# Merging two small loads, reordering the first norms and shortening a peeled pipeline in a two-stage graph network kernel

## The chip, the cores and the metric

The kernel runs on one core of a Trainium2 chip. The metric is the device time of one execution in microseconds (us). An execution before the change takes 4322.72 us (median of three runs, 4320.61 to 4323.55).

## The reference

`x` is 6250 nodes by 256 features, and `src` and `dst` name 100000 edges, sorted by `dst`. Cut to what matters, it computes:

```
h = relu(layernorm(x))
for W_self, W_neigh, b in three layers:          # the last without the relu
    mean = segment_sum(h[src], dst) / degree
    h = relu(h @ W_self + mean @ W_neigh + b)
x = x + h
h = relu(layernorm(x))
Q, K, V = h @ Wq + bq, h @ Wk + bk, h @ Wv + bv  # 8 heads of 32
s = sum(Q * K, per head) / sqrt(32)
a = softmax over each node's in-edges and itself of leaky_relu(s[src] + s[dst])
attn = segment_sum(a * V[src], dst)
h = batch_norm(h + attn @ Wo + bo)
h = batch_norm(h + relu(h @ W1 + b1) @ W2 + b2)
return x + h
```

## The kernel before

Nodes lie in 49 tiles of 128 (the last has 106), edges in 196 blocks (`NB`) of 512 (`BE`); the last block has 160 real edges. `HB` is `NB // 2`, 98.

**Setup.** ACT's queue loads the edge lists (`edges_scalar`, lines 325 to 336) into `raw_i`, one block to a partition, blocks 0 to 97 in the first half and 98 to 195 in the second. For each of `dst` and `src` it issues a DMA of 98 rows (L330), one of 96 rows (L331), one of a single row (L332) and one of 160 numbers (L333); then, behind a wait on GpSimd's memsets, two that fill the last row (L336). A full row is 2 KB. `walk_tables_vector` on DVE waits for all of them (`EDGE_DMAS` times 16 on `edges_in`) and turns the lists into the tables that every later loop reads. SP meanwhile loads `x` in six groups (`load_x`, L540; groups of 4, 9, 12, 12, 8 and 4 tiles), then the first layer's weights, then some edge values at the blocks' ends (L350 to L357; L351 and L352 are 97 rows of 8 bytes each). GpSimd gathers the rows of the first seven blocks straight from `x` (L664).

**First norm.** Each group of `x` ("x", 0 to 5) and each group of the seven gathered blocks ("r", 0 to 3, of 1, 2, 2 and 2 blocks, four rows' sets each) goes through `norm_stats_vector` on DVE, a square root on ACT (`root`, L623), `norm_fold_rows_vector` on DVE and a scaled relu on ACT (`norm`, L630), which for "x" also stores the rows to `h_table` (L634). Everything is in the order written out by hand in `norm_order`, `norm_x_vector`, `norm_ring_vector` and `norm_rows_scalar`: semaphores count along that order. On DVE `walk_tables_vector` stands between group "x" 0 and group "x" 1, and the "r" groups 1 to 3 come behind the first block's one-hots (`behind_first` of the first tile).

**The three layers.** GpSimd gathers the source rows of each block by four indirect DMAs (`gathers`, L763) into a ring of seven slots. It starts on `h_table` when all six stores are in and a slot is free. SP relays (`relay`): it tells PE that a block's rows have landed (L790) and GpSimd that a slot is free (L781). DVE makes one-hot matrices (L842), PE multiplies them with the rows (L897), and per tile come a mean (L952 to L957), transposes (L908, L911) and the dense products (L917, L920).

**The third layer** runs with the start of the attention stage as a software pipeline over tiles (`last_layer_step`). In step t PE sums tile t, finishes tile t-1, and projects tile t-3 (`project_tensor`: L1129 for Q and K, L1131 for V). DVE ends step t with `project_vector(t - 4)` (L1158 to L1172). `pipeline(eng, n, depth, step)` writes the first and last `depth` steps out and loops over those between. A wait of a peeled step on a number below 1 is dropped. In a loop it is always issued, on a register's value.

**Attention and feed-forward.** GpSimd gathers V rows (L1282), first from `vs_early` for five blocks, then from `vs_table`. DVE, ACT and PE do the softmax and the sums batch by batch. Feed-forward and both batch norms follow.

Of the kernel before, what the change touches and what calls it, by code (L numbers as in the profile page):

```python
# [42 lines left out]
def gnn_kernel(nc, x, src, dst, sage_w, sage_b, Wq, bq, Wk, bk, Wv, bv, Wo, bo, W1, b1, W2, b2,  # L43
# [6 lines left out]
    NT = -(-N // P)  # L50
    NP = NT * P
    NL = N - (NT - 1) * P
    NB = -(-E // BE)
# [35 lines left out]
    with ExitStack() as ctx:  # L89
# [230 lines left out]
        first_dmas, late_dmas = setup_dmas[0:3], setup_dmas[3:]  # L320
        FIRST_CONSTS, CONSTS = 16 * len(first_dmas), 16 * (len(setup_dmas) + 3)

        EDGE_DMAS, END_DMAS = 10, 8

        def edges_scalar(act):

            whole, rest = E // BE, E % BE
            for k, of in ((0, dst), (1, src)):
                rows = of[0:whole * BE].rearrange("(b e) -> b e", e=BE)
                act.dma_start(raw_i[:, k, 0, :], rows[0:HB]).then_inc(edges_in, 16)  # L330
                act.dma_start(raw_i[0:HB - 2, k, 1, :], rows[HB:NB - 2]).then_inc(edges_in, 16)  # L331
                act.dma_start(raw_i[HB - 2:HB - 1, k, 1, :], rows[NB - 2:NB - 1]).then_inc(edges_in, 16)  # L332
                act.dma_start(raw_i[HB - 1:HB, k, 1, 0:rest], of[whole * BE:E].rearrange("(a e) -> a e", a=1)).then_inc(edges_in, 16)  # L333
            act.wait_ge(pads_made, 3)
            for k in range(2):
                act.dma_start(raw_i[HB - 1:HB, k, 1, rest:BE], pads[:, 2 * k, rest:BE]).then_inc(edges_in, 16)  # L336
# [209 lines left out]
            sp.dma_start(h_nodes[0:NL, NT - 1, :], x[(NT - 1) * P:N, :]).then_inc(ln_in[-1], 16)  # L546

        raw_groups = [(0, 1)] + [(b, min(b + 2, RAW)) for b in range(1, RAW, 2)]
        norm_order = [("x", 0), ("x", 1), ("x", 2), ("x", 3), ("x", 4), ("x", 5), ("r", 0), ("r", 1), ("r", 2), ("r", 3)]
        assert len(norm_order) == len(ln_groups) + len(raw_groups)  # L550

        def norm_group(kind, g):
# [36 lines left out]
        def norm_x_vector(dve):  # L589

            dve.memset(h_nodes[:, NT - 1, :], 0.0).then_inc(pad_zero, 1)
            norm_stats_vector(dve, "x", 0)
            norm_fold_rows_vector(dve, "x", 0)
            walk_tables_vector(dve)
            norm_stats_vector(dve, "x", 1)
            norm_stats_vector(dve, "x", 2)
            norm_fold_rows_vector(dve, "x", 1)
            norm_stats_vector(dve, "x", 3)
            norm_fold_rows_vector(dve, "x", 2)
            norm_stats_vector(dve, "x", 4)  # L600
            norm_fold_rows_vector(dve, "x", 3)
            norm_stats_vector(dve, "x", 5)
            norm_fold_rows_vector(dve, "x", 4)
            norm_stats_vector(dve, "r", 0)
            norm_fold_rows_vector(dve, "x", 5)
            norm_fold_rows_vector(dve, "r", 0)

        def norm_ring_vector(dve):
            norm_stats_vector(dve, "r", 1)
            norm_stats_vector(dve, "r", 2)  # L610
            norm_fold_rows_vector(dve, "r", 1)
            norm_stats_vector(dve, "r", 3)
            norm_fold_rows_vector(dve, "r", 2)
            norm_fold_rows_vector(dve, "r", 3)

        def norm_rows_scalar(act):
            rows_out = by_partition(tables[0])

            def root(kind, g):
                at, _ = norm_place(kind, g)  # L620
                scale = norm_group(kind, g)[4]
                act.wait_ge(ln_var, at + 1)
                act.activation(scale, scale, ACT.Sqrt).then_inc(ln_sqrt, 1)  # L623

            def norm(kind, g):
                n, rows, _, _, scale, moved = norm_group(kind, g)
                at, _ = norm_place(kind, g)
                act.wait_ge(ln_fold, 2 * at + 2)
                for i in range(n):
                    act.activation(rows[i], rows[i], ACT.Relu, bias=moved[:, i:i + 1], scale=scale[:, i:i + 1]).then_inc(ln_done, 1)  # L630
                if kind == "x":
                    t0, t1 = ln_groups[g]
                    act.wait_ge(ln_done, t1)
                    act.dma_start(rows_out[:, t0:t1, :], h_nodes[:, t0:t1, :]).then_inc(stored0, 16)  # L634

            root("x", 0)
            norm("x", 0)
            root("x", 1)
            root("x", 2)
            norm("x", 1)  # L640
            root("x", 3)
            norm("x", 2)
            root("x", 4)
            norm("x", 3)
            root("x", 5)
            norm("x", 4)
            root("r", 0)
            norm("x", 5)
            norm("r", 0)
            root("r", 1)  # L650
            root("r", 2)
            norm("r", 1)
            root("r", 3)
            norm("r", 2)
            norm("r", 3)
            act.wait_ge(stored0, 16 * len(ln_groups))
# [218 lines left out]
        def sage_tensor(pe, l):  # L875
            if l == 0:
                walk_tables_tensor(pe)
                pe.wait_ge(walk_made, WALKED)
                pe.wait_ge(const_in, FIRST_CONSTS)

                pe.sem_inc(W["onehot_used"], BJ)
            else:
                pe.wait_ge(const_in, CONSTS)
                late_rows_tensor(pe, l)

            idle_ps = banks[:, 3 if l < 2 else 7, :]

            def sums(t):
                b0, b1 = span(pe, t)

                wait(pe, W["mean_made"], since("mean_made", l, t))
                pe.matmul(agg[:, 0:D + 1], zeros[:, 0:P], zeros[:, 0:D + 1], start=True, stop=False)
                with pe.Fori(b0, b1 + 1) as b:
                    pe.wait_ge(W["rows_ready"], since("rows_ready", l, b + 1))
                    for j in range(BJ):
                        pe.wait_ge(W["onehot_made"], since("onehot_made", l, (b + t) * BJ + j + 1))
                        pe.matmul(agg[:, 0:D + 1], onehot[:, j, :], ring[:, (b % SLOTS) * BJ + j, 0:D + 1],  # L897
                                  start=False, stop=False).then_inc(W["onehot_used"], 1)
                    for _ in range(4 if l < 2 else 1):
                        pe.matmul(idle_ps, zeros[:, 0:P], zeros[:], start=True, stop=True)  # L900
                pe.matmul(agg[:, 0:D + 1], zeros[:, 0:P], zeros[:, 0:D + 1], start=False, stop=True).then_inc(W["agg_done"], 1)  # L901

            def turn(t):

                wait(pe, W["lhs_made"], since("lhs_made", l, t))
                pe.wait_ge(W["self_made"], since("self_made", l, t + 1))
                for k in range(KD):
                    pe.transpose(tp[:, KD + k, :], h_self[:, k * P:(k + 1) * P], ident[:])  # L908
                pe.wait_ge(W["mean_made"], since("mean_made", l, t + 1))
                for k in range(KD):  # L910
                    last = pe.transpose(tp[:, k, :], mean[:, k * P:(k + 1) * P], ident[:])  # L911
                last.then_inc(W["turned"], 1)

            def products(t):

                wait(pe, W["h_made"], since("h_made", l, t))
                pe.matmul(dense[:, 0:D], ones_row[:], b_sage[0:1, l, :], start=True, stop=False)  # L917
                pe.wait_ge(W["lhs_made"], since("lhs_made", l, t + 1))
                for k in range(2 * KD):
                    last = pe.matmul(dense[:, 0:D], lhs[:, k, :], w_sage[:, l, k, :], start=False, stop=k == 2 * KD - 1)  # L920
                last.then_inc(W["out_done"], 1)

            def step(t):
                sums(t)
                turn(t)
                products(t)

            def last_layer_step(t):
                if there(t):
                    sums(t)  # L930
                if there(t - 1):
                    turn(t - 1)
                if there(t - 3):
                    turn_normed_tensor(pe, t - 3)
                if there(t - 1):
                    products(t - 1)
                if there(t - 3):
                    project_tensor(pe, t - 3)
            if l == 0:
                first_and_rest(pe, 2 * GS, step)  # L940
                late_ends_tensor(pe)
                with pe.Fori(2 * GS, NT) as t:
                    step(t)
            elif l == 1:
                first_and_rest(pe, NT, step)
            else:
                pipeline(pe, NT, 4, last_layer_step)

        def sage_vector(dve, l):
            def means(t):  # L950
# [173 lines left out]
        def project_tensor(pe, t):  # L1124
            pe.wait_ge(Q["lhs_made"], t + 1)
            wait(pe, Q["taken"], t)
            wait(pe, Q["step"], 4 * t - 3)
            for k in range(KD):
                pe.matmul(qk_ps, lhs_q[:, k, :], w_qkv[:, k, 0:2 * D], start=k == 0, stop=k == KD - 1)  # L1129
            for k in range(KD):  # L1130
# [995 lines left out]
```

## Time and profile before

| | |
|---|---|
| median of three runs | 4322.72 us |
| profiled execution | 4322.72 us, span 4320.9 us from first to last instruction |
| granted TensorE clock, mean | 0.945 |
| busy: PE, DVE, ACT, GpSimd | 82%, 50%, 11%, 70% |
| DMA, mean | 130 GB/s |

The span is what the trace shows; the 1.8 us around it are no part of it. PE's busy time includes products with zeros (L900) whose result nobody reads. GpSimd's busy time leaves out some 0.3 us between two indirect DMAs, so that 70% is a queue that hardly stops.

### The profile page before, as it was taken

What the parts mean: (1) busy time and instruction counts of PE and PEld (TensorE: products, weight loads), DVE (VectorE), ACT (ScalarE), POOL (GpSimd) and SP (SyncE); (2) the same over time, 40 slices, a digit from 0 to 9 for tenths busy, and PEclk for the clock granted to TensorE, in tenths of its full rate; (3) what the DMA queues carried; (4) which work ended last, traced back from release to release, by engine and by line L of the source; (5) the groups of instructions that cost most, each with busy time, mean ns of one, the idle gap of its engine ahead of it and who ended that gap; (6) DMA issues with size and microseconds to landing.
All of it is one profiled execution on the core that took longest, in us unless ns stands there. A gap on an engine that the chain in (4) does not pass through costs nothing. (4 is left out here: it accounts for less than half of the span.)

```text
span 4320.9 us, 79500 instructions
## 1 busy us (share of the span) xinstructions
PE 3542.6 (82%) x15834; PEld 2480.8 (57%) x15925; DVE 2155.8 (50%) x6078; ACT 487.9 (11%) x1111; POOL 3030.0 (70%) x3154
## 2 busy tenths in 40 slices
PE   4888888888988888888888888888777777777798
PEld 2666655555655556565666656665555555555544
DVE  5443333333333333333455555555577777777733
ACT  4000000000000000000010111101011111111122
POOL 5777777777777777777777777776777777777200
PEclk9999999999999999999999999999788989897999
DMA  5344334434344344344444444444655555554411
GB/s 197 119 138 124 120 110 125 124 105 143 106 123 124 104 124 124 104 124 126 128 141 136 138 140 136 139 139 147 168 147 156 147 156 148 159 147 137 127 60 60
DMA packets 284795, 563.69 MB, mean 130 GB/s; under 512 B 104637, under 2 KB 176132, under 8 KB 279690
## 3 DMA queue, kind: packets, MB, share of 16 engines
q0 software_dynamic: 150528, 414.45, 33.6%
q10 hardware_dynamic: 70180, 89.46, 6.2%
q1 hardware_dynamic: 63974, 58.59, 4.4%
q8 instruction: 33, 0.54, 0.1%
q14 instruction: 80, 0.66, 0.0%
HBM read 487.19 MB, written 73.45 MB: 130 GB/s over the span
## 5 line engine op out<-in xcount | busy, mean ns | idle before, releaser
L763 POOL DMA_INDIRECT arena<-h_table,idx_v x2292 | 2182.5, 952 | 731.7 <-issue 693.0
L897 PE MATMUL banks<-arena 128*128 x5856 | 1467.0, 395 | 356.2 <-SPq L790 244.8
L897 PEld LDWEIGHTS banks<-arena 128*128 128x128 f32 x5856 | 1110.7, 195 | 679.6 <-issue 497.8
L842 DVE TENSOR_SCALAR arena<-iota_t,dst_e 128x128 f32<-128x128 f32 x2928 | 853.5, 307 | 795.3 <-PE banks L897 515.2
L1282 POOL DMA_INDIRECT arena<-vs_table,idx_v x764 | 765.6, 1002 | 232.8 <-issue 229.4
L900 PE MATMUL banks<-zeros 128*128 128x512 bf16 x2108 | 585.3, 386 | 4.4 <-issue 0.4
L1500 PE MATMUL banks<-arena 128*128 x1952 | 518.5, 416 | 51.6 <-DVE arena L1844 51.5
L1500 PEld LDWEIGHTS banks<-arena 128*128 128x128 f32 x1952 | 366.4, 199 | 190.7 <-issue 119.2
L952 DVE TENSOR_SCALAR small<-banks 128x1 f32<-128x1 f32 x147 | 23.3, 159 | 674.4 <-PE banks L901 674.4
L900 PEld LDWEIGHTS banks<-zeros 128*128 128x128 bf16 x2196 | 218.7, 100 | 202.0 <-issue 12.7
L1020 ACT ACTIVATE lhs<-banks 128x512 f32<-128x512 f32 x147 | 87.8, 597 | 2137.9 <-PE banks L911 2137.7
L920 PE MATMUL banks<-arena,lhs 128*128 128x256 f32 x1176 | 293.2, 392 | 6.4 <-ACT lhs L1020 0.2
L1844 DVE SCALAR_TENSOR_TENSOR arena<-iota_n,tile_base,dst_e 128x256 f32<-128x256 f32 x488 | 224.2, 483 | 117.3 <-PE banks L1500 117.0
L920 PEld LDWEIGHTS banks<-arena,lhs 128*128 128x128 f32 x1176 | 211.7, 190 | 84.7 <-ACT lhs L1020 61.6
L1839 DVE TENSOR_TENSOR arena<-arena,banks (+1 forms) x196 | 239.1, 1220 | 30.9 <-issue 24.3
L911 PE MATMUL banks<-ident,tiles 128*128 128x128 f32 x294 | 63.3, 298 | 77.4 <-DVE tiles L957 77.4
L830 DVE TENSOR_SCALAR iota_t<-iota_n,tile_base 128x128 f32<-128x128 f32 x147 | 48.2, 328 | 153.7 <-issue 153.7
L917 PE MATMUL banks<-arena,ones_row 1*128 1x256 f32 x294 | 102.5, 428 | 0.0
L1129 PE MATMUL banks<-arena 128*128 128x512 f32 x196 | 92.3, 593 | 2.4 <-DVE arena L1162 2.4
L911 PEld LDWEIGHTS banks<-ident,tiles 128*128 128x128 f32 x294 | 33.3, 145 | 101.0 <-DVE tiles L957 101.0
L1972 PE MATMUL banks<-arena 128*128 (+2 forms) x208 | 86.2, 568 | 1.3 <-DVE arena L1927 1.3
L1982 PE MATMUL banks<-arena 128*128 128x512 f32 (+1 forms) x208 | 86.4, 569 | 0.2 <-DVE arena L1936 0.2
(265 smaller groups left out, 2512.3 us busy)
## 6 DMA issues: line engine op xcount, KB each, us to landing
arena<-h_table,idx_v POOLq DMA_INDIRECT x2292
arena<-dst_dram SPq DMA_DIRECT2D x14, 1792.0 KB
arena<-vs_table,idx_v POOLq DMA_INDIRECT x764
h_table<-arena ACTq DMA_DIRECT2D x11, 1024.0 KB, 7.4
h_early<-arena ACTq DMA_DIRECT2D x10, 1024.0 KB
vs_table<-arena ACTq DMA_DIRECT2D x49, 132.0 KB
x_dram<-arena ACTq DMA_DIRECT2D x49, 128.0 KB
hln_dram<-arena ACTq DMA_DIRECT2D x49, 128.0 KB
```

The costliest lines, as they stand in the source:

```text
L763: pool.indirect_dma_start(ring[:, s * BJ + j, 0:width], None, table, bass.IndirectOffsetOnAxis(idx_v[:, half, n * BJ + j:n * BJ + j + 1], ...
L842: dve.tensor_scalar(onehot[:, j, :], iota_t[:], dst_e[:, bass.ds(b * BJ + j, 1)], None, ALU.is_equal).then_inc(W["onehot_made"], 1)
L897: pe.matmul(agg[:, 0:D + 1], onehot[:, j, :], ring[:, (b % SLOTS) * BJ + j, 0:D + 1], start=False, stop=False).then_inc(W["onehot_used"], 1)
L900: pe.matmul(idle_ps, zeros[:, 0:P], zeros[:], start=True, stop=True)
L911: last = pe.transpose(tp[:, k, :], mean[:, k * P:(k + 1) * P], ident[:])
L917: pe.matmul(dense[:, 0:D], ones_row[:], b_sage[0:1, l, :], start=True, stop=False)
L920: last = pe.matmul(dense[:, 0:D], lhs[:, k, :], w_sage[:, l, k, :], start=False, stop=k == 2 * KD - 1)
L1129: pe.matmul(qk_ps, lhs_q[:, k, :], w_qkv[:, k, 0:2 * D], start=k == 0, stop=k == KD - 1)
L1282: pool.indirect_dma_start(v_ring[:, at, 0:VS], None, table, bass.IndirectOffsetOnAxis(idx_v[:, half, s * BJ + j:s * BJ + j + 1], 0)).then_ ...
L1500: pe.matmul(agg[:, 0:RW], onehot_v[:, j, :], v_ring[:, (b - (k - k % 2) * BB) * BJ + j, :], start=False, stop=False).then_inc(G["a_used"], 1)
L1839: dve.tensor_tensor(v, v, w.broadcast_to([P, BJ, HEADS, C]), ALU.mult).then_inc(G["rows_ready"], 1)
L1844: dve.scalar_tensor_tensor(onehot_v[:, j:j + 2, :], nodes_twice, tile_base[:, bass.ds(t, 1)], ends_of(b * BJ + j), ALU.add, ALU.is_equal). ...
```

## The change

There are three edits.

1. In `edges_scalar` the DMA of 96 rows and the one of a single row behind it become one of 97 rows, for `dst` and for `src`. Eight DMAs instead of ten are waited for.
2. In the first norm the statistics and roots of "r" 0 and "r" 1 move ahead of those of "x" 4 and "x" 5. ACT's relu work keeps its order. "r" 1 leaves `norm_ring_vector`.
3. PE's pipeline of the third layer peels three steps instead of four. The wait of `project_tensor` on DVE's steps becomes 4t instead of 4t-3 (the whole of `project_vector(t - 1)` instead of its first instruction).

```
-        EDGE_DMAS, END_DMAS = 10, 8
+        EDGE_DMAS, END_DMAS = 8, 8
...
-                act.dma_start(raw_i[0:HB - 2, k, 1, :], rows[HB:NB - 2]).then_inc(edges_in, 16)
-                act.dma_start(raw_i[HB - 2:HB - 1, k, 1, :], rows[NB - 2:NB - 1]).then_inc(edges_in, 16)
+                act.dma_start(raw_i[0:HB - 1, k, 1, :], rows[HB:NB - 1]).then_inc(edges_in, 16)
...
-        norm_order = [("x", 0), ("x", 1), ("x", 2), ("x", 3), ("x", 4), ("x", 5), ("r", 0), ("r", 1), ("r", 2), ("r", 3)]
+        norm_order = [("x", 0), ("x", 1), ("x", 2), ("x", 3), ("r", 0), ("r", 1), ("x", 4), ("x", 5), ("r", 2), ("r", 3)]
...
             norm_fold_rows_vector(dve, "x", 2)
+            norm_stats_vector(dve, "r", 0)
+            norm_fold_rows_vector(dve, "x", 3)
+            norm_stats_vector(dve, "r", 1)
+            norm_fold_rows_vector(dve, "r", 0)
             norm_stats_vector(dve, "x", 4)
-            norm_fold_rows_vector(dve, "x", 3)
+            norm_fold_rows_vector(dve, "r", 1)
             norm_stats_vector(dve, "x", 5)
             norm_fold_rows_vector(dve, "x", 4)
-            norm_stats_vector(dve, "r", 0)
             norm_fold_rows_vector(dve, "x", 5)
-            norm_fold_rows_vector(dve, "r", 0)
 
         def norm_ring_vector(dve):
-            norm_stats_vector(dve, "r", 1)
             norm_stats_vector(dve, "r", 2)
-            norm_fold_rows_vector(dve, "r", 1)
...
             norm("x", 2)
+            root("r", 0)
+            norm("x", 3)
+            root("r", 1)
             root("x", 4)
-            norm("x", 3)
             root("x", 5)
             norm("x", 4)
-            root("r", 0)
             norm("x", 5)
             norm("r", 0)
-            root("r", 1)
+            norm("r", 1)
             root("r", 2)
-            norm("r", 1)
...
-                pipeline(pe, NT, 4, last_layer_step)
+                pipeline(pe, NT, 3, last_layer_step)
...
-            wait(pe, Q["step"], 4 * t - 3)
+            wait(pe, Q["step"], 4 * t)
```

## Rows read from the trace of the kernel before

**Rows 1.** GpSimd's waits over the span: total us, times, longest us.
```profile
POOL arena L763 <- issue: 702.7, 2306, 0.3
...
POOL arena L763 <- SPq L781: 38.8, 18, 24.5
POOL arena L1282 <- DMA vs_early<-arena: 12.7, 1, 12.7
```

**Rows 2.** Lines 763 and 1282: duration ns min/median/max, first and last start us.
```profile
L763 POOL DMA_INDIRECT arena<-h_table,idx_v x2292: 942/946/1809, 66.0 to 2994.7; - x191
...
L1282 POOL DMA_INDIRECT arena<-vs_table,idx_v x764: 942/946/4050, 3034.5 to 4031.7; - x191
```

**Rows 3.** Timeline from 0 to 30 us: start us, us, engine, line, op, [idle before <-releaser].
```profile
1.87 0.35 ACTq L332 DMA_DIRECT2D arena<-in_dst_dram  x1
...
11.68 1.23 DVE L402 CAST arena<-arena 98x2048 f32<-98x2048 int32 x1 [2.43 <-DMA arena<-arena]
...
23.51 3.02 DVE L574 BATCH_NORM_STATS2 bn<-arena 128x6 f32<-128x256 f32 x9
```

**Rows 4.** DMA queues from 2.0 to 3.4 us: packets, MB, share of 16 engines.
```profile
q10 hardware_dynamic: 112, 0.20, 40.9%
```

**Rows 5.** DMA queues from 3.4 to 5.35 us.
```profile
q10 hardware_dynamic: 112, 0.20, 35.6%
```

**Rows 6.** DMA queues from 5.82 to 9.82 us.
```profile
q1 hardware_dynamic: 766, 0.78, 67.9%
q10 hardware_dynamic: 245, 0.40, 34.5%
```

**Rows 7.** DMA queues from 20 to 22 us.
```profile
q1 hardware_dynamic: 426, 0.44, 69.2%
q0 software_dynamic: 85, 0.25, 36.2%
```

**Rows 8.** DMA queues from 37.162 to 38.372 us.
```profile
q1 hardware_dynamic: 98, 0.00, 4.6%
```

**Rows 9.** Timeline of SP from 23.2 to 40 us.
```profile
30.40 5.80 SPq L352 DMA_DIRECT2D arena<-in_dst_dram  x1
```

**Rows 10.** Timeline from 30 to 110 us: first norm and the first blocks.
```profile
38.26 2.70 DVE L574 BATCH_NORM_STATS2 bn<-arena 128x6 f32<-128x256 f32 x8
...
44.92 5.99 ACT L630 ACTIVATE arena<-arena,shift,rstd 128x256 f32<-128x256 f32 x12
...
51.78 4.02 ACT L630 ACTIVATE arena<-arena,shift,rstd 128x256 f32<-128x256 f32 x8
...
58.80 2.07 ACT L630 ACTIVATE arena<-arena,bn 128x256 f32<-128x256 f32 x4 [0.41 <-ACT arena L630]
...
72.18 0.93 DVE L842 TENSOR_SCALAR arena<-iota_t,dst_e 128x128 f32<-128x128 f32 x4 [0.41 <-issue]
...
77.31 0.94 POOL L763 DMA_INDIRECT arena<-h_table,idx_v  x1 [6.63 <-SPq L781]
...
90.02 0.94 POOL L763 DMA_INDIRECT arena<-h_table,idx_v  x1 [3.01 <-SPq L781]
```

**Rows 11.** Waits from 2100 to 2990 us, in the third layer.
```profile
PE banks L897 <- SPq L790: 71.1, 38, 2.9
```

**Rows 12.** Timeline from 2500 us: a tile of the third layer.
```profile
2501.05 0.21 DVE L1169 TENSOR_SCALAR s_node<-small 128x8 f32 x1 [0.15 <-DVE small L1166]
2501.22 1.88 PE L1129 MATMUL banks<-arena 128*128 128x512 f32 x4
```

**Rows 13.** Timeline from 2985 us: the end of the third layer.
```profile
3014.79 1.96 PE L1129 MATMUL banks<-arena 128*128 128x512 f32 x4 [1.51 <-DVE arena L1162]
...
3015.51 0.33 DVE L1169 TENSOR_SCALAR s_node<-small 128x8 f32<-128x8 f32 x1
```

**Rows 14.** Timeline from 3026 us: the start of the attention stage.
```profile
3032.03 8.01 DVE L1251 TENSOR_SCALAR arena<-arena,node_id 128x512 f32<-128x512 int32 x20 [1.53 <-DMA vs_table<-arena]
...
3034.53 1.28 POOL L1282 DMA_INDIRECT arena<-vs_table,idx_v  x1 [0.30 <-issue]
```

## The prediction

> **What bounds the kernel now.** I read the waits of GpSimd first, then its two gather lines, then the timeline of the first 110 us, and last the third layer.
>
> GpSimd's waits are the key view [rows 1]. Nearly all its idle time in the three layers is "issue", 0.3 us between two gathers, which belongs to the stream itself. Of real waits there are 38.8 us for free slots, 24.5 of them one wait, and 12.7 us at the hand-over to the attention stage. The gather lines [rows 2] show one stream: from 66.0 to 2994.7 us there are 2323 intervals (2292 gathers from the table and 32 from the early copies, less one), and 2928.7 / 2323 = 1.26 us is one gather of 0.946 us with its 0.3. So the layers take what GpSimd needs, and whatever moves the stream's start moves its end by as much. The attention stage hangs on layer 2's end and so on the same start. The reader is to see that the end of the kernel is set 4250 us earlier: by when GpSimd gets going.
>
> What sets that is the timeline of the start. DVE begins `walk_tables_vector` at 11.68 us, released by the last edge DMA [rows 3]. From there DVE goes without a pause to 23.51, where the statistics of "x" 1 begin, and the norms follow. GpSimd's first gather from the table is at 65.99, released by the slot of block 0; it waits again until 77.31 and 90.02 [rows 10], and then runs. So the edge DMAs stand at the head of the critical path.
>
> **Edit 1, the edge loads.** What it removes is two issues on ACT's queue of about 0.35 us each (one is L332 in [rows 3]); if nothing else changed, the two pad DMAs behind them would start and land up to 0.7 us earlier.
>
> What it adds is a shape. A DMA leaves one packet for each row and one small one for each DMA engine that reports its share done. In 2.0 to 3.4 us the 98-row DMA left 112 packets, 98 + 14 [rows 4]; in 3.4 to 5.35 us the 96-row one left 112, 96 + 16 [rows 5]. So 98 rows went over 14 engines, 7 each, and 96 over 16, 6 each. The kernel already has two loads of 97 rows, though of 8 bytes: L351 and L352 [rows 9]. The first left 98 packets in 37.162 to 38.372 us [rows 8]: 97 + 1. One engine did it all. 97 is prime, and 98 = 14 x 7; the rows say that the number of engines divides the number of rows. So I expect each merged load to put its 97 rows on a single engine, and both loads on the same one, since they are of one shape.
>
> The Trainium skill says so too, and speaks against the edit by it: "DMA: Bandwidth & Descriptors", "Why a DMA increments its semaphore by 16 and not by 1", has the largest number up to 16 that divides the slowest dimension of both sides, and the lowest-numbered engines take the work. Its 127-partition example goes on one engine, as 97 would. The same page gives an engine about 27 GiB/s; by that the 426 KB below would take some 15 us, below the floor from rows.
>
> How long does this take? That engine gets 7 + 97 full rows for `dst` and as many for `src`, 208 rows of 2 KB. Floor: in [rows 4] 40.9% of 16 engines over 1.4 us is 9.2 us for 98 rows, 0.094 us each; 208 of them are 19.5 us. But SP's `x` loads share every engine. Ceiling: in [rows 6] the `src` loads, 13 rows to an engine, took the 4.0 us, 0.31 us a row; 208 would be 64 us. Between them I count the engine's work. A packet of `x` (1 KB) is 0.679 x 64 / 766 = 0.057 us [rows 6]. The engine's part of `x` is 48 full tiles x 8 rows, 53 of the last tile's 106 (two engines by the same rule), and 32 of the weights, 469 packets, 26.6 us. A gather's 4 KB packet is 0.362 x 32 / 85 = 0.136 us [rows 7], 28 raw gathers x 2 = 56 of them, 7.6 us. Together 53.7 us, from 2.2 us on: by 56 nothing is left. If the engine turns between the queues at equal bytes, two packets of `x` go with each row: 208 x (0.094 + 0.114) + 7.6 = 51 us, ending at 53. The shares in [rows 6] and [rows 7] add to 102 and 105%, so packets overlap a little; I take the last row at 50 us, and 45 to 56 as its own range. From the last row to DVE's start it was 11.68 - 9.82 = 1.9 us, kept. DVE then starts at 51.9 instead of 11.7: +40.2 us.
>
> What else is queued there: ACT's later issues may block while the ring is full, as SP's L352 did for 5.80 us behind L351 [rows 9]. ACT's root and relu of "x" 0 come behind them, but have until 51.9. The `x` groups are in the same engine's other queue; group 1 is wanted at 51.9 + 11.8 = 63.7, when the engine is empty. None of this adds. Nothing hides the 40 us: everything on GpSimd from its 66 us on waits for this chain.
>
> **Edit 2, the first norm.** In the old clock. "r" 0 and 1 take 2.0 and 3.6 us of DVE statistics (eight, with aggregation, as from 38.26 [rows 10]). DVE gets to "x" 4 only behind the fold of "r" 0, whose root stands behind ACT's relu of "x" 2: 45.4. It ends there at 49.0, then must fold "r" 1, whose root stands behind the relu of "x" 3, which ends at 50.9 [rows 10]: 52.2. Then the statistics of "x" 5, 2.0 us, to 54.2. ACT has the root of "x" 5 ahead of the relu of "x" 4, so this relu starts at 54.7 instead of 51.78: +2.9. "x" 5 and "r" 0 follow: block 0 is ready at 63.7 instead of 60.9 (58.80 + 2.07), and GpSimd's first gather comes at 68.8. But the "r" 1 relu follows at once, to 67.7, and behind the first one-hots DVE has only "r" 2 and 3, 7.2 us of statistics from 58.0, and their roots, which stand behind ACT's "r" 1 relu: 68.8. Block 1's one-hots come at 69.2 instead of 72.18. PE follows with blocks 1, 2 and 3 in the same steps, so GpSimd's other two starts come 3.0 us earlier, 74.3 and 87.0; block 7's four gathers are done at 73.8. The last of the three sets the stream: -3.0 us. Bounds: -3.0, and +2.9 if the first start should bind, which it doesn't while the third lies where it does.
>
> **Edit 3, the pipeline.** The order of PE's instructions stays; one peeled step becomes a loop step. The new wait holds PE until L1169 of the tile before has ended, 2501.26, where PE's L1129 began at 2501.22 [rows 12]: with a semaphore's way about +0.3 us a tile. PE waited 71.1 us for rows in 38 waits of 890 us [rows 11], up to 2.9 each, so this is hidden. In the written-out tail it costs once or twice the full difference, from 14.79 to 15.84 [rows 13], together some 2 us. The last store to `vs_table` released DVE at 3032.03, and GpSimd wants it only at 3034.2 [rows 14]: 2.2 us of slack. Taken as nothing, at most +2. Without the cover it would be 45 x 0.3 = 13.5 us more.
>
> **The sum**, against the profiled execution's own 4322.72 us, which is also the median: 4322.7 + 40.2 - 3.0 + 0 = 4360 us.
>
> **The rivals.**
> (a) One engine, but the edge rows are served ahead of `x`. For it: a ring that always has work may get more than half the turns. Against: [rows 6], where these rows had a third of the engines. Last row between 22 and 40 us, time 4332 to 4348, middle 4340.
> (b) The merged load spreads, as 2 KB rows might be cut otherwise than 8-byte ones. Then the head moves by -0.7 us and edit 2 by -3.0: 4319 us, no change that can be measured. Against: 98 and 96 rows of 2 KB were split by whole rows. It decides from two engines or more: 97 rows on two would already cost half.
> (c) The new wait of PE makes it the bound of the third layer: 4360 + 15 = 4375 us. Against: [rows 11].
> (d) More is stuck than the edges: SP's issues behind the full ring (weights, the late end values) come after 62 us and hold PE or the relay, or edit 2 costs its +2.9: 4366 to 4385.
>
> **How the numbers follow.** Forecast 0.70, (a) 0.13, (b) 0.06, (c) 0.03, (d) 0.08. 0.2% is 8.6 us, about what a measurement of this kernel can tell from no change. Slower is all but (b) and a sliver of (a): 0.91; same 0.07; faster 0.02. The forecast's own range is 4353 to 4366. The 8-in-10 range reaches into (a) and (d): 4338 to 4374.
>
> **What would show it.** DVE's L402 near 52 us, released by a DMA, is edit 1; if at 11 to 12, (b). The DMA queues between 12 and 48 us should show ACT's queue with some 190 packets where it now has only stores. Relative to L402, GpSimd's first three starts should come +2.8, -3.0 and -3.0 us against 54.3, 65.6 and 78.3. In the third layer PE's L1129 should begin about 0.3 us later after L1162, and GpSimd's waits beyond 100 us stay as they are. The prediction is wrong if the edge rows do not go to one engine, or if that engine serves them in far less than 0.2 us each.

## The result and the profile after

The changed kernel takes 4344.88 us (median of five runs, 4341.93 to 4345.54), against 4322.39 us (4320.61 to 4323.55) for the one before: 1.0051 times as long, 95% interval 1.0037 to 1.0066. That is slower, by 22.5 us, as forecast in kind. It lies inside the 8-in-10 range of 4338 to 4374 us, but 15 us under the forecast value and outside its own range of 4353 to 4366, at the time of rival (a). The profiled run took 4346.55 us with a span of 4344.7, 23.8 us more than before's span. Lines from L332 on stand one number lower than before.

GpSimd's waits (total us, times, longest us), which answer to [rows 1]:

```profile
POOL arena L762 <- issue: 704.0, 2311, 0.3
...
POOL arena L762 <- SPq L780: 59.0, 12, 55.2
POOL arena L1281 <- DMA vs_early<-arena: 12.7, 1, 12.7
...
POOL arena L1281 <- DMA vs_table<-arena: 4.1, 1, 4.1
```

Its two gather lines (duration ns, first and last start us), which answer to [rows 2]:

```profile
L762 POOL DMA_INDIRECT arena<-h_table,idx_v x2292: 942/946/1806, 95.5 to 3015.6; - x191
...
L1281 POOL DMA_INDIRECT arena<-vs_table,idx_v x764: 942/946/6032, 3058.3 to 4055.2; - x191
```

The stream is unchanged between its ends: the same "issue" of 0.3 us, now 2311 times. Its first gather starts 29.5 us later, its last only 20.9 us later (3015.6 against 2994.7). So 8.6 us are won back at the start. Then 2.9 us are lost between the last gather of the layers and the first from `vs_table` (42.7 us against 39.8), behind which stands a wait of 4.1 us that is new. What comes after moves by 23.5 us (its last gather) to 23.8 us (the end).

The timeline from 0 to 62 us (start us, us, engine, line, op, idle before and its releaser) shows the start of the chain, [rows 3] before:

```profile
4.69 17.64 ACTq L332 DMA_DIRECT2D arena<-in_src_dram  x1
...
38.97 1.23 DVE L401 CAST arena<-arena 98x2048 f32<-98x2048 int32 x1 [12.99 <-DMA arena<-arena]
...
50.75 3.02 DVE L573 BATCH_NORM_STATS2 bn<-arena 128x6 f32<-128x256 f32 x9
```

DVE's walk begins at 38.97 instead of 11.68, +27.3 us, and the statistics of "x" 1 keep their distance to it (11.8 us both times). Three windows of the DMA queues (packets, MB, share of 16 engines) show why. The first is 3.4 to 5.35 us, that of [rows 5]:

```profile
q1 hardware_dynamic: 568, 0.51, 90.6%
q10 hardware_dynamic: 20, 0.04, 6.5%
```

The second is 12 to 20 us:

```profile
q1 hardware_dynamic: 1263, 1.28, 50.2%
q0 software_dynamic: 388, 1.07, 40.4%
q10 hardware_dynamic: 43, 0.08, 2.9%
```

Where ACT's queue (q10) moved 112 packets in 1.95 us, it now moves 20, and then 43 in 8 us: 0.19 us a row, on 2.9% of the sixteen engines, less than half of one engine. That fits one engine which carries the rows and spends over half its time on the other queues. The third is 20 to 22 us:

```profile
q0 software_dynamic: 63, 0.17, 31.9%
q10 hardware_dynamic: 13, 0.02, 3.3%
q1 hardware_dynamic: 13, 0.01, 1.9%
```

SP's queue (q1) with `x` moved 426 packets in this window before [rows 7] and now moves 13, exactly as many as ACT's. The two together took 5.2% of sixteen engines, 0.83 of one. So `x` too has come down to the pace of one engine, and that engine takes one `x` packet (0.047 us) for one packet of the edges (0.081 us).

The timeline from 60 to 125 us, the first blocks, which answer to the second half of [rows 10]:

```profile
81.41 4.04 ACT L629 ACTIVATE arena<-arena,shift,rstd 128x256 f32<-128x256 f32 x8
...
88.34 6.00 ACT L629 ACTIVATE arena<-arena,bn 128x256 f32<-128x256 f32 x12 [0.41 <-ACT arena L629]
...
90.77 3.79 PE L896 MATMUL banks<-arena 128*128 x8 [35.32 <-SPq L789]
...
95.52 0.94 POOL L762 DMA_INDIRECT arena<-h_table,idx_v  x1 [55.20 <-SPq L780]
95.61 0.97 DVE L841 TENSOR_SCALAR arena<-iota_t,dst_e 128x128 f32<-128x128 f32 x4 [0.41 <-issue]
96.11 2.00 PE L896 MATMUL banks<-arena 128*128 x8 [0.28 <-DVE arena L841]
...
111.05 0.94 POOL L762 DMA_INDIRECT arena<-h_table,idx_v  x1 [0.78 <-SPq L780]
```

Counted from the walk's start, GpSimd's first start comes at +56.5 us (before +54.3), block 1's one-hots at +56.6 (before +60.5), its last start at +72.1 (before +78.3). GpSimd no longer waits at its second start. There is a second gain beside the earlier one-hots: block 1's products take 2.00 us. Before, the timeline had them at half that speed, after a pause of PE:

```profile
72.68 3.79 PE L897 MATMUL banks<-arena 128*128 x8 [5.96 <-DVE arena L842]
```

The windows view (us, busy us of PE, PEld, DVE, ACT, POOL, granted clock, DMA share, GB/s) gives the granted clock there, before:

```profile
72.00:77.00 5.00, 4.32 (x10) 2.98 (x11) 2.08 (x8) 5.00 (x11) 0.00 (x0) 0.50 0.00 0
```

and after:

```profile
95.00:98.00 3.00, 2.72 (x12) 1.72 (x11) 2.00 (x8) 3.00 (x7) 1.89 (x2) 1.00 0.14 44
```

0.50 is the level of 1.2 GHz, 1.00 that of 2.4 GHz. From block 1's products to block 2's, PE took 5.09 us before and takes 2.70 now.

The end of the third layer, on the timeline from 3015 us, which answers to [rows 13] and [rows 14]:

```profile
3036.78 3.00 PE L1128 MATMUL banks<-arena 128*128 128x512 f32 x4 [2.64 <-DVE s_node L1168]
...
3039.57 1.71 PE L1130 MATMUL banks<-arena 128*128 128x256 f32 x4
...
3043.53 2.93 PE L1128 MATMUL banks<-arena 128*128 128x512 f32 x4 [2.03 <-DVE s_node L1168]
...
3046.26 1.78 PE L1130 MATMUL banks<-arena 128*128 128x256 f32 x4
...
3058.28 1.07 POOL L1281 DMA_INDIRECT arena<-vs_table,idx_v  x1 [4.14 <-DMA vs_table<-arena]
```

The waits before the last two projections are 2.64 and 2.03 us, now on DVE's L1168 (before 1.51 and 0.89, on L1162), and the products behind them are longer, 3.00 and 2.93 us against 1.96, and 1.71 and 1.78 against 1.03. The windows view gives their clock:

```profile
3036.00:3040.00 4.00, 3.22 (x5) 1.50 (x6) 1.09 (x5) 0.60 (x1) 3.09 (x4) 0.69 0.60 168
```

Before, the two windows of 4 us from 3014 to 3022 have 1.00. The balance in the profiled runs: +27.3 at the walk (edit 1), -6.3 from there to GpSimd's third start (edit 2), so the stream's end at +20.9; the hand-over +2.9; the end of the kernel 23.8 us later.

### The profile page after: what moved, and what is told of

Same layout as the page of the kernel before. It is cut to its first block and busy times, and to the rows that moved or that the text cites. A ratio compares the mean times of both kernels' runs of the same rounds, so it can differ in the third digit from the quotient of the medians.

```text
span 4344.7 us, 79597 instructions
## 1 busy us (share of the span) xinstructions
PE 3546.9 (82%) x15924; PEld 2471.0 (57%) x15925; DVE 2157.0 (50%) x6078; ACT 488.6 (11%) x1111; POOL 3027.9 (70%) x3154
## 5 line engine op out<-in xcount | busy, mean ns | idle before, releaser
L899 PE MATMUL banks<-zeros 128*128 128x512 bf16 x2196 | 604.5, 385 | 0.0
L1128 PE MATMUL banks<-arena 128*128 128x512 f32 x196 | 98.5, 626 | 4.7 <-DVE s_node L1168 4.7
```

## The experiments

They ran on other chips. The kernel before itself takes some 6350 to 6430 us there instead of 4322. In the experiments' profiles the mean granted clock is 0.78 to 0.79 (0.945 before), and GpSimd waits 1443 to 1495 us for slots (38.8 in [rows 1]). A difference of a few us is not to be had from such totals, so the verdicts rest on rows of the start and of the tail. Where a total is given, it is the median of 10 or 12 runs beside the kernel before on the same chip. The others are single runs. "First start" is GpSimd's first gather from `h_table`, "one-hots" are those of block 1, and both are often counted from the start of DVE's walk.

**e1_edges: edit 1 alone.**

```
-        EDGE_DMAS, END_DMAS = 10, 8
+        EDGE_DMAS, END_DMAS = 8, 8
...
-                act.dma_start(raw_i[0:HB - 2, k, 1, :], rows[HB:NB - 2]).then_inc(edges_in, 16)
-                act.dma_start(raw_i[HB - 2:HB - 1, k, 1, :], rows[NB - 2:NB - 1]).then_inc(edges_in, 16)
+                act.dma_start(raw_i[0:HB - 1, k, 1, :], rows[HB:NB - 1]).then_inc(edges_in, 16)
```

> Edit 1 alone. Theory 1: the 97 rows of both loads go through one DMA engine, each row waiting its turn beside x's; DVE's first step of the walk comes at 39 us instead of 11.7 and everything behind keeps its distances: 4322.4 + 27.3 = about 4350 us. Rival: the late start in the changed kernel comes in part from the new order of the norms; then the first step of the walk comes clearly before 39 us, and the time stays under 4345 us.

6450.22 us, 1.0029 times before (95% 1.0005 to 1.0054): 24.6 us longer, with an interval of 3 to 35 us. The timeline:

```profile
4.68 17.61 ACTq L332 DMA_DIRECT2D arena<-in_src_dram  x1
...
39.23 1.23 DVE L401 CAST arena<-arena 98x2048 f32<-98x2048 int32 x1 [13.62 <-issue]
...
92.99 0.94 POOL L762 DMA_INDIRECT arena<-h_table,idx_v  x1 [52.41 <-SPq L780]
...
99.73 3.79 PE L896 MATMUL banks<-arena 128*128 x8 [6.85 <-DVE arena L841]
```

Edit 1 by itself gives the whole delay of the walk. From the walk on, the old distances stand (first start +53.8, before +54.3), and block 1's products take 3.79 us, as before.

**e2_norms and e2_norms_b: edit 2 alone**, on two chips. The diff is that of `norm_order`, `norm_x_vector`, `norm_ring_vector` and the ACT list in the change; only the line that matters most:

```
-        norm_order = [("x", 0), ("x", 1), ("x", 2), ("x", 3), ("x", 4), ("x", 5), ("r", 0), ("r", 1), ("r", 2), ("r", 3)]
+        norm_order = [("x", 0), ("x", 1), ("x", 2), ("x", 3), ("r", 0), ("r", 1), ("x", 4), ("x", 5), ("r", 2), ("r", 3)]
```

> Edit 2 alone. Theory 1 (order and clock): block 1's one-hots come early enough that PE has no long gap before block 1, its clock stays at full and the products of block 1 take 2.0 us instead of 3.8; the third start of GpSimd comes 6 us earlier against the walk, 4316 us. Rival (order alone): only the 3 us of the one-hots are won, 4319 us.

> Edit 2 alone once more, as the first chip took some 2100 us longer for every kernel and its times can't tell a few us. Theory 1 (order and clock): PE's clock stays full for block 1 and the third start of GpSimd comes 6 us earlier against the walk, 4316 us. Rival (order alone): 3 us, 4319 us.

Totals: 0.9997 (0.9978 to 1.0016) and 1.0009 (0.9984 to 1.0034), no difference. The timeline of the first, from 60 to 95 us:

```profile
81.70 0.94 POOL L763 DMA_INDIRECT arena<-h_table,idx_v  x1 [40.53 <-SPq L781]
81.79 0.97 DVE L842 TENSOR_SCALAR arena<-iota_t,dst_e 128x128 f32<-128x128 f32 x4 [0.41 <-issue]
82.29 2.00 PE L897 MATMUL banks<-arena 128*128 x8
...
87.54 0.29 DVE L842 TENSOR_SCALAR arena<-iota_t,dst_e 128x128 f32<-128x128 f32 x1 [2.83 <-PE banks L897]
...
90.39 0.32 DVE L842 TENSOR_SCALAR arena<-iota_t,dst_e 128x128 f32<-128x128 f32 x1 [2.57 <-remote]
...
93.25 0.49 DVE L842 TENSOR_SCALAR arena<-iota_t,dst_e 128x128 f32<-128x128 f32 x2 [2.54 <-remote]
...
94.00 0.94 POOL L763 DMA_INDIRECT arena<-h_table,idx_v  x1 [2.60 <-SPq L781]
```

Against e3_pipe, which has the old order, and counted from each one's walk: first start +70.3 against +67.6, one-hots +70.4 against +73.8, block 1's products 2.00 us against 3.44. Edit 2 does in the start what the changed kernel shows; on the second chip block 1's products take 2.04 us. What it wins is gone again at block 3, whose one-hots wait twice for some 2.5 us on "remote", a releaser outside the core's own record, which the profile after does not have there. So these totals neither confirm nor deny its 6.3 us.

**e3_pipe: edit 3 alone.**

```
-                pipeline(pe, NT, 4, last_layer_step)
+                pipeline(pe, NT, 3, last_layer_step)
...
-            wait(pe, Q["step"], 4 * t - 3)
+            wait(pe, Q["step"], 4 * t)
```

> Edit 3 alone. Theory 1: the wait on the whole of DVE's projection steps costs in the written-out tail, PE's gaps lower its clock there, the last store to vs_table comes some 5 us later and uses up 2 us of slack; GpSimd waits 3 to 4 us there: 4325 to 4327 us. Rival: the tail has slack enough and the 4.1 us wait in the changed kernel comes from something else: 4322 us, no wait.

6428.78 us, 0.9994 (0.9971 to 1.0017). The last two projections:

```profile
4495.80 1.96 PE L1129 MATMUL banks<-arena 128*128 128x512 f32 x4 [2.26 <-issue]
...
4500.82 1.95 PE L1129 MATMUL banks<-arena 128*128 128x512 f32 x4 [1.98 <-issue]
```

The waits are near those of the changed kernel (2.64 and 2.03); the products are not slower. So slow products are no fixed consequence of the wait.

**e4_norms_pipe: edits 2 and 3 together**, without edit 1 (their diffs as above).

> Edits 2 and 3 without edit 1. If the three edits add up: 4322.4 - 6.3 + 3 = about 4319 us. If they act on each other (x arriving late together with the new order of the norms): several us off this.

6429.68 us, 1.0000 (0.9979 to 1.0020). First start 81.81, one-hots 81.90: the start of e2. Waits of 2.52 and 2.13 us in the tail, and the last L1129 takes 3.57 us. In these rows the edits don't disturb each other.

**e5_dst_only: the merged load for `dst` alone**, to tell an engine that serves rows one after another from a fixed delay.

```
-        EDGE_DMAS, END_DMAS = 10, 8
+        EDGE_DMAS, END_DMAS = 9, 8
...
+                if k == 0:
+                    act.dma_start(raw_i[0:HB - 1, k, 1, :], rows[HB:NB - 1]).then_inc(edges_in, 16)
+                else:
+                    act.dma_start(raw_i[0:HB - 2, k, 1, :], rows[HB:NB - 2]).then_inc(edges_in, 16)
+                    act.dma_start(raw_i[HB - 2:HB - 1, k, 1, :], rows[NB - 2:NB - 1]).then_inc(edges_in, 16)
```

> Only the dst load merged to 97 rows, the src load as before. Theory (one engine, 208 rows in some 36 us, 0.17 us a row): the engine has 7 + 97 + 7 + 6 = 117 rows, the last at about 22 us, and DVE's first step of the walk comes at 23 to 25 us, half way between 11.7 and 39. Rival (the late start comes from ACT's blocked issues, not from the engine's rows): nothing blocks ACT with one such load, and the walk begins before 15 us.

```profile
23.59 1.23 DVE L405 CAST arena<-arena 98x2048 f32<-98x2048 int32 x1 [8.12 <-DMA arena<-arena]
```

Less the 1.9 us from last row to DVE and the 2.2 us at the start, both taken from the kernel before, that is 19.5 us for the 7 + 97 + 7 + 6 = 117 rows of the loaded engine, 0.167 us each. The changed kernel has 38.97 - 4.1 = 34.9 us for 208 rows, 0.168 each. The delay is proportional to the rows on the one engine. ACT's queue isn't held here (its longest issue is 1.66 us).

**e6_two_parts: the same 97 rows as 48 and 49**, still two issues.

```
-                act.dma_start(raw_i[0:HB - 2, k, 1, :], rows[HB:NB - 2]).then_inc(edges_in, 16)
-                act.dma_start(raw_i[HB - 2:HB - 1, k, 1, :], rows[NB - 2:NB - 1]).then_inc(edges_in, 16)
+                act.dma_start(raw_i[0:48, k, 1, :], rows[HB:HB + 48]).then_inc(edges_in, 16)
+                act.dma_start(raw_i[48:HB - 1, k, 1, :], rows[HB + 48:NB - 1]).then_inc(edges_in, 16)
```

> The same 97 rows as two loads of 48 and 49 rows, no load of a single row. Theory (the number of engines divides the number of rows): 16 and 7 engines, at most 3 + 7 = 10 rows of 2 KB on one engine in place of 97; the walk begins at 12 to 14 us. Rival (these rows are slow for another reason, the last rows of the list or the partitions they go to): it begins near 39 us as in the changed kernel.

```profile
12.17 1.24 DVE L402 CAST arena<-arena 98x2048 f32<-98x2048 int32 x1 [3.29 <-DMA arena<-arena]
```

The same bytes go to the same rows, and the delay is 0.5 us instead of 27. Even that is none that can be told: with the old edge loads the walk starts between 11.34 and 12.27 us in eight profiles. It is the count 97 that costs. "DMA: Bandwidth & Descriptors" of the Trainium skill, section "Why a DMA increments its semaphore by 16 and not by 1", takes the largest number up to 16 that divides the slowest dimension of both sides; by that rule 48 rows go to 16 engines and 49 to 7. This run agrees with it as far as the walk's start can.

**e7_x_behind: edit 1, with SP's `x` groups 1 to 5 held until the edges are in**, to measure what the other queue takes of the loaded engine.

```
+            sp.wait_ge(edges_in, 16 * EDGE_DMAS)
             for g in range(1, len(ln_groups)):
                 load_x(sp, g)
```

> Edit 1 with the loads of x groups 1 to 5 held back until the edges are in. Theory (each row waits one turn of x's queue): without x the engine needs 0.09 us a row and the gathers' share, 208 rows in 20 to 27 us, and the walk begins at 24 to 30 us instead of 39. Rival (the engine is slow by itself on such rows, whatever else is queued): it stays at 37 us or more.

```profile
4.52 11.16 ACTq L332 DMA_DIRECT2D arena<-in_src_dram  x1
...
27.51 1.27 DVE L401 CAST arena<-arena 98x2048 f32<-98x2048 int32 x1 [8.47 <-DMA arena<-arena]
```

208 rows in 27.51 - 4.1 = 23.4 us, 0.113 each. With `x` beside them (e1, same edit) the walk starts 11.7 us later. Some 3.3 of these are gathers, whose queue took 28.5% of the engines in e1 from 2 to 37 us. Add the 32 packets of `x` group 0 that this run has too, some 1.5 us, and `x` comes to about 9.9 us in e1, an estimate: 0.048 us a row. One `x` packet takes 0.047 us in the third window of the profile after (0.057 by [rows 6]). So about one packet of `x` went with each row, not two, as that window counts it directly.

**e11_root5: edit 2 with the root of "x" 5 behind the relu of "x" 4**, meant to take back the later first start.

```
-            root("x", 5)
             norm("x", 4)
+            root("x", 5)
             norm("x", 5)
```

> Edit 2 with the root of x 5 moved behind ACT's relu of x 4, so that this relu need not wait for the statistics of x 5. Against edit 2 alone, counted from the walk's first step: the relu of x 4 starts 2 to 3 us earlier, block 0's products and GpSimd's first start 2 us earlier, the one-hots of block 1 2 us earlier. Rival: ACT then waits for DVE's folding of x 5 instead, and nothing is won.

First start 81.69 (e2 81.70), one-hots 83.09 (e2 81.79). The theory fell and the rival was near: ACT's relu of "x" 4 waits 2.61 us for DVE's fold of "x" 4 (L587), which stands behind the statistics of "x" 5, so ACT gains nothing by asking later.

**e12_after: the changed kernel itself**, on the chip of the next two.

> The changed kernel itself on the chips of these experiments, where the kernel before takes some 6400 us. Theory: the walk begins 27 us late as before, but here DVE's own start is held up for 13 us by other things when the walk is early, so that less of the 27 us reaches GpSimd: GpSimd's first start some 13 to 18 us later than without the edits, the time 10 to 25 us longer. Rival: the 22 us of the first measurement come back unchanged.

6358.12 us, 1.0004 (0.9970 to 1.0039): no difference there that can be told, where +10 to +25 us were expected; these lie in the interval too. Its start is nevertheless that of the changed kernel:

```profile
39.59 1.23 DVE L401 CAST arena<-arena 98x2048 f32<-98x2048 int32 x1 [14.19 <-DMA arena<-arena]
...
96.23 0.95 POOL L762 DMA_INDIRECT arena<-h_table,idx_v  x1 [55.29 <-SPq L780]
...
96.82 2.00 PE L896 MATMUL banks<-arena 128*128 x8 [0.69 <-DVE arena L841]
```

Walk to first start is 56.6 us, as in the profile after. But in e3_pipe, whose walk is early, DVE is held up between the two:

```profile
35.48 0.86 DVE L577 BATCH_NORM_AGGREGATE bn<-bn 128x2 f32<-128x6 f32 x8 [3.69 <-remote]
37.56 0.18 DVE L577 BATCH_NORM_AGGREGATE bn<-bn 128x2 f32<-128x6 f32 x1 [1.21 <-issue]
...
42.74 0.18 DVE L577 BATCH_NORM_AGGREGATE bn<-bn 128x2 f32<-128x6 f32 x1 [2.17 <-issue]
...
45.69 0.18 DVE L579 TENSOR_SCALAR rstd<-bn 128x12 f32<-128x12 f32 x1 [2.77 <-remote]
```

Such stalls fall between 32 and 46 us. A kernel whose DVE is then waiting for the edges loses nothing by them, so that here the 27 us of edit 1 reach GpSimd's first start as 13.7 (92.99 in e1, 79.25 in e3). What the long stream with its many waits makes of these 13.7 us is not shown: edit 1 alone cost 3 to 35 us in total (e1), the whole change between -19 and +25 (e12).

**e8_wait_only: the wait of edit 3, four steps still peeled**.

```
-            wait(pe, Q["step"], 4 * t - 3)
+            wait(pe, Q["step"], 4 * t)
```

> The stronger wait of PE alone (4t), with four peeled steps as before. Theory: the wait and not the peeling costs; at the end of the third layer PE's first product of the last two projections waits for DVE's L1169 and begins 1 us later than with the old wait, as in edit 3 alone, where PE sat idle 2.3 and 2.0 us before them. Rival: the loop's step in place of the written-out one is what shifts PE; then the waits stay at 0.9 to 1.5 us.

Waits of 1.98 and 2.64 us before the last two projections. The first of the two tells the kernels apart: 0.94, 1.17, 1.27, 1.40, 1.48, 1.49 and 1.51 us in seven runs with the old wait (both of edit 2 alone, e11, e7, e6, e1, e5), and 1.98, 2.26, 2.30 and 2.52 us in the four with the new one (e8, e3, e12, e4), whether three steps are peeled or four. The wait acts, the peeling doesn't. What reaches GpSimd can't be read here: its wait before the first gather from `vs_table` is 2.5 to 12.4 us in kernels with the old wait and 8.5 to 10.1 in those with the new one.

**e9_tail_weak: edits 2 and 3, but the old wait in the written-out steps** (three steps peeled, edge loads as before).

```
-            wait(pe, Q["step"], 4 * t - 3)
+            wait(pe, Q["step"], 4 * t - 3 if isinstance(t, int) else 4 * t)
```

> Edits 2 and 3 with the old wait (4t-3) kept in the written-out last steps, where t is a number. Theory: PE's waits before the last two projections go back to 0.9 to 1.5 us and end with DVE's L1162. With edit 2's earlier third start this is the version that I would take: 6 us below the kernel before, if a time could tell that here. Rival: the waits stay above 2 us.

6339.54 us, 0.9974 (0.9946 to 1.0002), and waits of 1.13 and 2.83 us. The first is back among those of the old wait. The second says nothing: with the old wait everywhere it is 0.94, 1.89, 2.57, 3.19, 3.64, 5.46 and 5.79 us. This is the best candidate: by the two profiles of the result it should keep the 6.3 us of the start without edit 3's part of the tail. It is not shown to be faster than the kernel before, as the interval reaches over 1.

## Why the prediction was right, and where it was not

**What bounds the kernel: right.** The stream kept its pace and moved as a whole (20.9 us at its last gather, 23.5 at the last of the attention stage). The chain from edge loads through DVE's walk to the first start held to the microsecond: 11.8 us from walk to "x" 1.

**Edit 1, one engine: right.** The walk waited on a DMA; two parts of 48 and 49 rows cost 0.5 us (e6); the merged load for one list cost 11.9 us (e5), less than half. The window from 20 to 22 us fits it: both queues together hold 0.83 of one engine. Rival (b) is out. The sign that the prediction named for it, q10 busy with edge rows where it had only stores, is there (43 packets from 12 to 20 us).

**Edit 1, the size: the step that failed.** It is "If the engine turns between the queues at equal bytes, two packets of `x` go with each row". With two, 0.094 + 0.114 = 0.208 us a row and the walk at 51.9. Measured were 0.168 us a row for everything that the engine did, gathers included, and the walk at 38.97. The window from 20 to 22 us of the profile after has one packet of `x` for one of the edges, and e1 against e7 gives the same. One packet in the prediction's own sum gives 208 x (0.094 + 0.057) + 7.6 = 39 us from 2.2 on, and a walk at some 43. The other 4 us are two sizes and an overlap. The packets took less than [rows 4] and [rows 6] had them, 0.081 and 0.047 us in that window: 4.8 us less. The gathers took more, 29.0% of the engines from 2 to 37 us, 10.2 us for each: the 0.136 us from [rows 7] is a mean over 85 packets of 0.25 MB, some 3 KB each, and was put on full packets of 4 KB. That makes 208 x (0.081 + 0.047) + 10.2 = 36.8 us against 34.9; the last 2 us may be the overlap of packets that the prediction names. The prediction had the right number in its own rows and chose against it. [Rows 6], read per packet, have 766 of `x` to 245 of the edges, but over all sixteen engines, where the `x` queue also had engines without edge rows waiting; the ratio says nothing of an engine on which both always wait. The time that came out is that of rival (a), 4332 to 4348, and so is the last row, at 37.1 us (its 22 to 40). Its words, "served ahead of `x`", describe it half: neither queue went first; each took about one packet in turn, and the row's packet is the larger.

The Trainium skill had this: "DMA: Bandwidth & Descriptors", "Queues, rings and completion order", lets each engine take turns between its queues by packets, not by bytes. It counts a packet there as several descriptors, 9 to 17; the runs here can't show that grouping, only that the counts came out equal, 13 and 13 packets from 20 to 22 us.

**ACT's queue: right, and free.** The issue behind the second merged load (the 160 numbers, L332) was held for 17.64 us; nothing on ACT was due before 38.97. With `x` held back it was 11.16 us, and with one merged load no issue took over 1.7 us.

**Edit 2: right in kind, half too small.** First start forecast +2.8, measured +2.2. One-hots of block 1 forecast -3.0, measured -3.9. The step that was mis-sized is "PE follows with blocks 1, 2 and 3 in the same steps": it didn't take the same steps, as block 1's products ran at a granted clock of 1.00 instead of 0.50. From block 1 to block 2 PE took 2.70 us instead of 5.09, another -2.4. Together -6.3 at the last start. The pause of PE that went with the low clock, 5.96 us before, was in the timeline of [rows 10] too, at its 72.68 us, and the shift of +2.8 and -3.0 leaves next to nothing of it; that was to be had from the trace. That edit 2 does it is shown by the runs with the old order, 3.44 to 3.79 us in e1, e3, e5, e6, e7 and e8, against 2.00 to 2.33 us in e2, e2_norms_b, e4, e9, e11 and e12.

**Edit 3: in the steady state right, in the tail too small.** The loop cost nothing that can be seen: GpSimd's stream has no new wait, and PE's waits for rows in the third layer are 71.4 us (71.1 in [rows 11]). Rival (c) is out. Of the forecast 0.3 us a tile the one tile compared, at 2501 us before and 2522 after, shows 0.1: L1128 begins 1.6 us after the start of L1161, where L1129 began 1.5 us after that of L1162. The step "together some 2 us [...] 2.2 us of slack. Taken as nothing, at most +2" measured otherwise: DVE's release by the last `vs_table` store moved from 3032.03 to 3057.56, 25.5 us, 4.6 more than the stream, and 2.9 of it came through. The waits grew by 2.3 us, as forecast. The products behind them, at a clock of about 0.7, took 2.0 us more in L1128 and 1.4 in L1130, which the prediction didn't have. That the new wait costs some 1 us before the last projection but one is shown by eleven runs (under e8). That the slow products come from it is not: e3 has the waits and products of 1.96 us; e4, e8, e9 and e12 have only the last one slow (2.88 to 3.57 us); and so have e1, e5, e7 and e11 without edit 3, 3.44, 2.40, 2.56 and 3.70 us behind waits of 5.46, 2.57, 3.64 and 5.79 us. So of the 2.9 us at the hand-over, which one profile shows, about 1 is edit 3's by experiment and the rest only goes with it. It was not tried to keep PE busy in those gaps.

**The sum** with what was measured: 4322.7 + 27.3 - 6.3 + 2.9 = 4346.6 us, the profiled run's own time. Of the 13.4 us from there to the forecast, 12.9 are edit 1, 3.3 edit 2, and 2.9, with the other sign, the tail. That the last two nearly cancel is luck, and the time fell inside the 8-in-10 range because that range made room for rival (a).

Open stays the cause of the stalls on the other chips, the change's price there beyond the interval of e12, and the part of the clock in the tail. No run has the old wait in a loop with three steps peeled: its first turn, for tile 0, would wait for the value 4 x 0 - 3 = -3.

## What to carry to other kernels

Before two loads are merged to save an issue, count into how many equal shares the merged row count splits: here two loads of 97 rows went to one engine and cost 27 us where 98, 96, 48 and 49 rows did not, and a saved issue is one of 0.35 us. If one engine must serve two queues, count the packets of both in a window in which that engine alone is behind, as from 20 to 22 us here, and price its turns by that: one for one in this kernel. And when a reordering fills a gap of the TensorE, count the products behind the gap again at the other clock level: 2.4 of the 6.3 us of edit 2 came from there.

## What the runs showed of the hardware

An engine with both queues waiting took one 2 KB row in 0.168 us, the gathers' packets included, and in 0.113 us with most of `x` held back; e5 and the changed kernel agree on the first figure to 1%, for 117 and 208 rows. From 20 to 22 us of the profile after it moved 13 packets of each queue, 0.081 us for one of the edges and 0.047 us for one of `x`.

A DMA issue can hold its engine's queue until some of the rows ahead have gone: the issue behind the `src` load took 17.64, 17.61 and 17.07 us in three profiles with both loads merged, 11.16 us with `x` held back, and 1.14 us where `dst` alone was merged. At the average pace of each, an estimate, the issue ended in the changed kernel and in e7 when the loaded engine had moved about 120 of its 208 rows: (22.33 - 2.2) / 0.168 = 120 and (15.68 - 2.2) / 0.113 = 119. e5 has 117 rows in all and never gets there.

The granted clock doesn't tell all of a product's time. Block 0's products took 3.79 us after an idle stretch of PE of 35 us, in a window that shows a granted clock of 1.00:

```profile
90.00:95.00 5.00, 4.23 (x10) 2.97 (x11) 1.91 (x14) 4.63 (x12) 0.00 (x0) 1.00 0.02 7
```

Block 1's, with as many instructions, took the same 3.79 us at 0.50 and 2.00 us at 1.00. Whether the record lags behind what the engine gets after a long idle, or something else slows these products, is not shown.

The same kernel took 4322 us in the runs of the result and some 6350 to 6430 us in those of the experiments, with DVE and GpSimd held up many times in the stretch of the layers. The change's 0.5% in the first was 0.04% in the second, with an interval from -0.3 to +0.4%. Distances within the start could still be compared, totals could not.
